# A graph network on one core: one-hots made once a group, a fused key compare, and another split of edge groups between two layers

## The chip, the core and the metric

One core of a Trainium2 chip runs the whole program as one launch. The metric is the device time of one execution in microseconds, the median over runs.

## The reference, cut to what matters

A graph of 6250 nodes with 206250 edges (sorted by `dst`; 128 features a node, 128 attributes an edge). Both layers gather node rows by edge and sum them by node:

```python
h = relu(layernorm(x))
deg = segment_sum(w, src) + 1                      # self loops added
msg = dinv[src] * w * dinv[dst] * (h @ kernel)[dst]
x = x + relu(segment_sum(msg, src) + bias)         # first layer
h = relu(layernorm(x))
m_fwd  = concat(h[src], edge_attr) @ W_fwd  + b_fwd    # summed by dst
m_back = concat(h[dst], edge_attr) @ W_back + b_back   # summed by src
agg = (segment_sum(m_fwd, dst) + segment_sum(m_back, src)) / count
x = x + layernorm(leaky(agg) + h) * gamma + beta   # second layer
```

So beside the sums over node rows there are two sums of edge attributes, by `src` and by `dst`, which both layers' passes collect.

## The kernel before

An edge group is 8 chunks of 128 edges (`J = 8`, `GE = 1024`); there are `NG = 202`. A supertile is 256 destination nodes; there are `SUPER = 25`. The stages, each a block of its own in which the five engines run their own instruction streams and meet at semaphores:

1. `setup_and_degrees` counts degrees, writes the edge records `d.rec` (source, destination, offset in the window, weight), the keys and the offsets.
2. `dst_lists` gathers, for each node, its edges' sources (50 columns) and, for the nodes from `S0` supertiles on, their weights (`near_w`, 2 x `DS` columns); POOL gathers them by indirect DMA, TensorE turns them.
3. `first_layer`, called the pass here. `G1 = GPI * (2 * DS + 1)` groups are walked in slots of `GPI` groups. For a chunk j of group g, VectorE makes three 128x128 matrices of ones and zeros: `spread_hot` (which window row an edge's destination is), `same` (which edges of the chunk have the same source) and `sum_hot` (like `spread_hot`, turned). TensorE spreads the window's rows over the edges (L838), adds the attributes by destination into the window bank (L852), and sums payload and attributes of edges with one source (L856, L857). ScalarE copies the sums (L929). POOL scatters the 128 rows of a chunk by an indirect DMA that adds in memory (L705). VectorE's `add_window` (L721) adds the window bank to `attr_sums`. The nodes of the last `DS` supertiles get their node sums in another way, by matrices: beside the groups of one slot, half a supertile is done: one-hots (`one_hots`, `weigh`; L776, L777, L782), batches of products that count edges for pairs (`pairs`, L888), turns (L866), a product with node rows (L878) and an addition to `gcn_t` (`add_up`, L791). These are dealt out over the slot's `C = GPI * J` chunk steps at a distance of `STRIDE = GPI // 2` steps. Weights of edges that go to those nodes are set to zero in the pass, so `G1` groups must cover all edges of the first `S0` supertiles.
4. `gcn_nodes` merges the four tables of sums and ends the first layer.
5. `dense_sums`, the second layer's node sums, by matrices for all 25 supertiles (called tiles here). The `NB = NG - G1` groups that are left run beside it: `PG` ahead of the first tile, then `GL = 4` beside each of `BT = (NB - PG) / GL` tiles; these lack payload and spread. Their tables are then loaded and merged (L1513, L1547) while the other tiles run.
6. `last_nodes` ends the second layer.

In each stream the order is fixed by the code. VectorE prepares group g + 1 (`prepare`) in the chunk steps of group g; step j waits until TensorE has summed chunk j of group g (`summed`, in the second layer `chunk_done`). SyncE loads a group's records (`rec`), offsets (`rel_b`), keys (`key_b`), window and attributes into two buffers each. ScalarE's `sums` hold two groups. A duplicate is told by an edge's earlier neighbours with its key (`before`): such an edge's row goes to a spare row.

## Time and profile before

| | |
|---|---|
| median of 3 runs | 4742.2 us (4732.38 to 4747.09) |
| the profiled execution: its time, its span | 4736.39 us, 4734.6 us |
| mean granted TensorE clock | 0.888 |
| busy: TensorE, VectorE, ScalarE, POOL | 73%, 79%, 39%, 60% |
| pass: first scatter to end of the last | 710.4 to 2702.0 us |
| second layer: first scatter, last tile's end | 2904.6, 4545 us |

Busy times count only work: semaphore, register and DMA-issuing instructions of an engine are left out, except POOL's indirect DMAs, whose span is the making of descriptors. "Idle before" a group is the time in which its engine did nothing ahead of its instructions, with what ended the idle. In a timeline the first number is the start in us, the second the duration; durations of VectorE overlap a little, so costs are read from start to start.

### The profile page before, as it was taken

The page shows a single profiled execution, that of the slowest core. Times are in us where ns is not written, and L with a number is a line of the kernel's source. Part 1 is how long each engine was busy: PE and PEld are TensorE (multiplying, and loading weights), DVE is VectorE, ACT ScalarE, POOL GpSimd, SP SyncE. Part 2 cuts the span into 40 slices and gives each one's busy share as a digit, 9 for nine tenths or more (in the row PEclk, how much of TensorE's full clock was granted, in tenths as well). Part 3 has the DMA queues.
Part 4 walks back from the last instruction along what each step waited for, and adds up shares of the span by engine and source line. Part 5 has one row for each costly group of instructions (what it writes and reads, how often), then busy time and mean ns, then how long its engine had stood idle before and what let it go on. Part 6 is the DMA issues. An engine that isn't in the chain of part 4 may idle for free. (4 is left out here: it accounts for less than half of the span.)

```text
span 4734.6 us, 104535 instructions
## 1 busy us (share of the span) xinstructions
PE 3462.1 (73%) x30910; PEld 2929.9 (62%) x31114; DVE 3722.4 (79%) x11962; ACT 1851.2 (39%) x4574; POOL 2819.5 (60%) x1705
## 2 busy tenths in 40 slices
PE   3555317888887888778888523798888888998955
PEld 3445217777776767677777422677777777776645
DVE  8999729998889888898899445887878777864527
ACT  1011004544444444444444313444444444455513
POOL 0000168888888888888888603787777777860000
PEclk8777659998989999999899766899999999999977
DMA  9990118888878777887788785455555555557031
GB/s 170 315 104 0 43 37 144 144 139 141 142 136 143 139 137 139 141 142 140 134 141 141 124 142 122 72 83 80 81 77 81 81 82 79 82 78 84 4 89 28
DMA packets 679953, 518.82 MB, mean 110 GB/s; under 512 B 305948, under 2 KB 592548, under 8 KB 677736
## 3 DMA queue, kind: packets, MB, share of 16 engines
q0 software_dynamic: 256640, 183.99, 34.6%
q1 hardware_dynamic: 422724, 327.85, 28.7%
q8 instruction: 263, 4.31, 0.4%
q14 instruction: 326, 2.67, 0.2%
HBM read 288.51 MB, written 249.53 MB: 114 GB/s over the span
## 5 line engine op out<-in xcount | busy, mean ns | idle before, releaser
L705 POOL DMA_INDIRECT gcn_sums<-fl_sums,fl_to_i x1008 | 1655.0, 1642 | 362.5 <-issue 160.2
L1531 POOL DMA_INDIRECT gcn_sums<-shared,ds_to_i x608 | 1038.0, 1707 | 486.6 <-ACT shared L1781 306.8
L929 ACT COPY fl_sums<-bank 128x256 f32<-128x256 f32 x1008 | 378.0, 376 | 662.2 <-PE bank L857 571.2
L1736 PE MATMUL bank<-ds_counts,ds_parts 128*128 128x256 bf16 x3675 | 595.5, 275 | 0.0
L852 PE MATMUL bank<-fl_sum_hot,fl_attrs 128*128 128x128 f32 x2016 | 404.9, 307 | 169.5 <-DVE attr_sums L721 169.4
L1805 ACT COPY ds_turned<-bank 128x1024 bf16<-128x1024 bf16 (+1 forms) x325 | 313.1, 963 | 537.7 <-PE bank L1721 534.7
L852 PEld LDWEIGHTS bank<-fl_sum_hot,fl_attrs 128*128 128x128 f32 x2016 | 328.3, 210 | 300.0 <-issue 259.9
L1769 ACT CAST ds_counts<-bank 128x392 bf16<-128x392 f32 x800 | 379.1, 491 | 234.9 <-PE bank L1679 222.0
L371 PE MATMUL bank<-places,row_hot 128*128 128x200 bf16 x1616 | 267.6, 292 | 255.4 <-DVE places L324 255.4
L856 PE MATMUL bank<-fl_pay,fl_same 128*128 128x128 f32 x2016 | 420.5, 292 | 30.2 <-DVE fl_same L741 23.1
L742 DVE SCALAR_TENSOR_TENSOR fl_earlier<-fl_key_b,fl_pat,before_me 128x128 bf16<-128x128 bf16 x1008 | 442.0, 439 | 0.0
L1756 PE MATMUL bank<-ds_turned,ds_now 128*128 128x512 bf16 (+1 forms) x1746 | 411.9, 365 | 10.9 <-issue 0.2
L838 PE MATMUL bank<-fl_window,fl_spread_hot 128*128 128x128 f32 x2016 | 294.9, 291 | 166.7 <-DVE fl_spread_hot L735 166.1
L922 ACT ACTIVATE fl_pay<-bank,fl_weight 128x128 f32<-128x128 f32 x1008 | 288.3, 369 | 326.6 <-PE bank L838 326.4
L857 PE MATMUL bank<-fl_attrs,fl_same 128*128 128x128 f32 x2016 | 410.8, 287 | 0.0
L1664 DVE TENSOR_TENSOR src_sums<-src_sums,bank 128x512 f32<-128x512 f32 (+1 forms) x325 | 212.1, 654 | 213.8 <-PE bank L1756 210.2
L838 PEld LDWEIGHTS bank<-fl_window,fl_spread_hot 128*128 128x128 f32 x2016 | 256.5, 199 | 196.2 <-DVE fl_spread_hot L735 164.1
L371 PEld LDWEIGHTS bank<-places,row_hot 128*128 128x128 bf16 x1616 | 194.0, 120 | 287.9 <-DVE places L324 276.3
L741 DVE TENSOR_SCALAR fl_same<-fl_key_b,fl_pat 128x128 f32<-128x128 bf16 x1008 | 351.8, 349 | 18.5 <-PE bank L857 16.0
L856 PEld LDWEIGHTS bank<-fl_pay,fl_same 128*128 128x128 f32 x2016 | 329.6, 204 | 54.1 <-issue 46.0
L735 DVE TENSOR_SCALAR fl_spread_hot<-fl_rel_b,part 128x128 f32<-128x128 bf16 x1008 | 359.1, 356 | 2.1 <-DMA fl_rel_b<-dst_offset 1.4
L1736 PEld LDWEIGHTS bank<-ds_counts,ds_parts 128*128 128x128 bf16 x3675 | 334.9, 99 | 29.7
(238 smaller groups left out, 8098.5 us busy)
## 6 DMA issues: line engine op xcount, KB each, us to landing
fl_attrs<-in_edge_attr SPq DMA_DIRECT2D x126, 512.0 KB, 4.6
shared<-in_edge_attr SPq DMA_DIRECT2D x150, 256.0 KB
fl_rel_b<-dst_offset SPq DMA_DIRECT2D x126, 256.0 KB
fl_key_b<-src_key SPq DMA_DIRECT2D x126, 256.0 KB
gcn_sums<-zeros SPq DMA_DIRECT2D x40, 640.0 KB
...
gcn_sums<-fl_sums,fl_to_i POOLq DMA_INDIRECT x1008
...
```

The source lines that it names most:

```text
L371: nc.tensor.matmul(hist[:, 0:4 * NT], row_hot[:, h, 0, j, :], col_w[:, h, j, :, :].rearrange("p s n -> p (s n)"), **ends)
L705: nc.gpsimd.indirect_dma_start(out=d.tab_gcn[j % K], out_offset=bass.IndirectOffsetOnAxis(ap=to_i[:, (GPI * kk + gi) % 4, j:j + 1], axis=0 ...
L742: counted = nc.vector.scalar_tensor_tensor(earlier[:, j, :], key_p[:, h, :, j], pat_f[:, j:j + 1], d.before_me[:], ALU.is_equal, ALU.mult, ...
L838: last = nc.tensor.matmul(row_bank[:, q * F:(q + 1) * F], spread_hot[:, half * U + q, :], window[:, h, :], start=True, stop=True)
L852: nc.tensor.matmul(win_bank[:, 0:P], attrs[:, h, jj, :], sum_hot[:, jj, :], start=(jj == 0), stop=(jj == J - 1))
L856: nc.tensor.matmul(sum_bank[j % 2][:, 0:F], same[:, j, :], pay[:, j // U, j % U, :], start=True, stop=True)
L857: nc.tensor.matmul(sum_bank[j % 2][:, F:2 * F], same[:, j, :], attrs[:, h, j, :], start=True, stop=True).then_inc(summed, 1)
L929: nc.scalar.copy(sums[:, h, j, :], sum_bank[j % 2][:, 0:2 * F]).then_inc(staged, 1)
L1531: nc.gpsimd.indirect_dma_start(out=d.tab_gcn[j % K].rearrange("n (two f) -> (n two) f", two=2), out_offset=bass.IndirectOffsetOnAxis(ap=to ...
L1736: ins = nc.tensor.matmul(row_bank[:, 0:2 * P], parts[:, tile, s, :], counts[:, h, tile, :, :].rearrange("p b q -> p (b q)"), start=(tile = ...
L1756: ins = nc.tensor.matmul(back_bank[v][:, 0:n], now[:, h, half, s, :], turned[:, v, half, 0:n], start=(half == 0 and s == 0), stop=(half == ...
L1769: nc.scalar.copy(to, pair_bank[batch % B][:, 0:PB * HH].rearrange("p (c k) -> p k c", c=PB)).then_inc(pair_copied, 1)
```

## The change

`S0` goes from 15 to 12 and `GPI` from 6 to 4, so `DS` is 13 instead of 10, the pass has 108 groups in 27 slots of 4 instead of 126 in 21 slots of 6, and 94 groups instead of 76 run in the second layer: `PG` = 6 ahead of it and 4 beside each of 22 tiles, not 18. `STRIDE` falls from 3 to 2.

On VectorE `same` is now made by the instruction that also counts: the compare is multiplied by `from_me` (key positions from the edge's own on) and summed, so `same` is triangular and the last edge of a key gets the whole sum; the separate `earlier` is gone. `spread_hot` is made by one instruction a group at step j = 2, `sum_hot` by one a group (`spot_sums`) at the group's first step, which waits until the group before is summed. The target indices need one instruction less in the pass.

```diff
@@ -62,14 +62,14 @@
 TILES = ROWS // P
 HI = -(-N // P)
 SUPER = TILES // 2
-S0 = 15
+S0 = 12
 DS = SUPER - S0
 DST0 = S0 * 2 * P
-GPI = 6
+GPI = 4
 G1 = GPI * (2 * DS + 1)
 NB = NG - G1
 GL = 4
-PG = 4
+PG = 6
 BT = (NB - PG) // GL
 PAIRS = P
 HH = 2 * HI
...
@@ -674,9 +674,11 @@
                     g, h = group(i, kk, gi), gi % 2
                     at_least(sp, to_ready, g - 1)
                     sp.sem_inc(load_turns, 1)
-                    sp.dma_start(flat(rec[:, h, :, :]), d.rec[bass.ds(g, 1), :, :].rearrange("o p r -> (o p) r")).then_inc(rec_in[h], 16)
                     sp.dma_start(flat(rel_b[:, h, :, :]), everywhere(d.dst_offset, g)).then_inc(rel_in[h], 16)
                     sp.dma_start(flat(key_b[:, h, :, :]), everywhere(d.src_key, g)).then_inc(key_in[h], 16)
+                    at_least(sp, sum_ready, g - 1)
+                    sp.sem_inc(load_turns, 1)
+                    sp.dma_start(flat(rec[:, h, :, :]), d.rec[bass.ds(g, 1), :, :].rearrange("o p r -> (o p) r")).then_inc(rec_in[h], 16)
                     at_least(sp, summed, J * (g - 1))
                     sp.sem_inc(load_turns, 1)
                     base = sp.value_load(d.base_i[0:1, bass.ds(g, 1)], min_val=0, max_val=N)
...
@@ -712,6 +714,12 @@
 
         @block.vector
         def _(dve):
+            def spot_sums(g, h):
+
+                at_least(dve, summed, J * g)
+                nc.vector.tensor_tensor(sum_hot[:], d.iota[:].unsqueeze(1).to_broadcast([P, J, P]), rec[:, h, 2, :].unsqueeze(2).to_broadcast([P, J, P]),
+                                        ALU.is_equal).then_inc(sum_ready, 1)
+
             def add_window(g):
 
                 at_least(dve, summed, J * (g + 1))
...
@@ -729,31 +737,24 @@
                     nc.vector.scalar_tensor_tensor(weight[:, h, :], rec[:, h, 1, :], DST0 - 0.5, rec[:, h, 3, :], ALU.is_lt, ALU.mult).then_inc(weight_ready, 1)
                     nc.vector.tensor_tensor(to_f[:], d.spare[:], rec[:, h, 0, :], ALU.subtract)
                     nc.vector.tensor_scalar(pat[:], rec[:, h, 0, :], PAT, 65536.0, ALU.add, ALU.mult).then_inc(step, 1)
-                    dve.wait_ge(rel_in[h], 16 * loads(i, kk, gi))
-                if ahead and j % U == 0:
-                    dve.wait_ge(row_ready, 2 * (g - 1) + j // U + 1)
-                nc.vector.tensor_scalar(spread_hot[:, j, :], rel_b[:, h, :, j], d.part[:, 0:1], None, ALU.is_equal).then_inc(spread_ready, 1)
-                if j == 0:
                     dve.wait_ge(key_in[h], 16 * loads(i, kk, gi))
-                    dve.wait_ge(step, 4 * g + 1)
+                    dve.wait_ge(step, 2 * g + 1)
                 if ahead:
                     dve.wait_ge(summed, J * (g - 1) + j + 1)
-                nc.vector.tensor_scalar(same[:, j, :], key_p[:, h, :, j], pat_f[:, j:j + 1], None, ALU.is_equal).then_inc(same_ready, 1)
-                counted = nc.vector.scalar_tensor_tensor(earlier[:, j, :], key_p[:, h, :, j], pat_f[:, j:j + 1], d.before_me[:],
-                                                         ALU.is_equal, ALU.mult, accum_out=before[:, j:j + 1])
+                nc.vector.scalar_tensor_tensor(same[:, j, :], key_p[:, h, :, j], pat_f[:, j:j + 1], d.from_me[:],
+                                               ALU.is_equal, ALU.mult, accum_out=later[:, j:j + 1]).then_inc(same_ready, 1)
+                if j == 2:
+                    dve.wait_ge(rel_in[h], 16 * loads(i, kk, gi))
+                    at_least(dve, row_ready, 2 * g)
+                    nc.vector.tensor_scalar(spread_hot[:], rel_b[:, h, :, :].rearrange("p q j -> p j q"), d.part[:, 0:1], None,
+                                            ALU.is_equal).then_inc(spread_ready, 1)
                 if j == J - 1:
-                    counted.then_inc(step, 1)
-                for jj in (range(4) if j == 3 else range(j, j + 1) if j > 3 else ()):
-                    nc.vector.tensor_scalar(sum_hot[:, jj, :], d.iota[:], rec[:, h, 2, jj:jj + 1], None, ALU.is_equal).then_inc(sum_ready, 1)
-                if j == J - 1:
-                    dve.wait_ge(step, 4 * g + 2)
-                    nc.vector.scalar_tensor_tensor(to_f[:], before[:], 0.0, to_f[:], ALU.is_gt, ALU.mult).then_inc(step, 1)
-                    dve.wait_ge(step, 4 * g + 3)
-                    nc.vector.tensor_tensor(to_f[:], to_f[:], rec[:, h, 0, :], ALU.add).then_inc(step, 1)
-                    dve.wait_ge(step, 4 * g + 4)
+                    dve.wait_ge(same_ready, J * (g + 1))
+                    nc.vector.scalar_tensor_tensor(to_f[:], later[:], 1.5, to_f[:], ALU.is_gt, ALU.mult).then_inc(step, 1)
+                    dve.wait_ge(step, 2 * g + 2)
                     for k in range(K):
                         at_least(dve, added[k], 16 * per_table * (g - 3))
-                    nc.vector.tensor_copy(to_i[:, (GPI * kk + gi) % 4, :], to_f[:]).then_inc(to_ready, 1)
+                    nc.vector.tensor_tensor(to_i[:, (GPI * kk + gi) % 4, :], to_f[:], rec[:, h, 0, :], ALU.add).then_inc(to_ready, 1)
                     dve.wait_ge(to_ready, g + 1)
 
             in_twos = lambda a: a.rearrange("p q (c two) -> p q c two", two=2)
...
@@ -804,6 +805,8 @@
                 more = not (isinstance(i, int) and i == DS)
                 for c in range(C):
                     gi, j = divmod(c, J)
+                    if j == 0:
+                        spot_sums(group(i, kk, gi), gi % 2)
                     if j == 0 and not (first and gi == 0):
                         add_window(group(i, kk, gi) - 1)
                     if not (last and gi == GPI - 1):
...
@@ -830,7 +833,7 @@
             def spread(i, kk, gi, half):
 
                 g, h = group(i, kk, gi), gi % 2
-                pe.wait_ge(spread_ready, J * g + U * (half + 1))
+                pe.wait_ge(spread_ready, g + 1)
                 if half == 0:
                     pe.wait_ge(window_in[h], 16 * loads(i, kk, gi))
                 at_least(pe, paid, J * g + U * half)
...
@@ -846,8 +849,7 @@
                     pe.wait_ge(attr_in[h], 16 * loads(i, kk, gi))
                 if j == 2:
                     at_least(pe, window_added, g)
-                if j >= 2:
-                    pe.wait_ge(sum_ready, ch + 1)
+                    pe.wait_ge(sum_ready, g + 1)
                 for jj in (range(3) if j == 2 else range(j, j + 1) if j > 2 else ()):
                     nc.tensor.matmul(win_bank[:, 0:P], attrs[:, h, jj, :], sum_hot[:, jj, :], start=(jj == 0), stop=(jj == J - 1))
                 pe.wait_ge(same_ready, ch + 1)
...
@@ -1449,9 +1450,10 @@
             pair_of_tiles(BT // 2 - 1, 1, True, False)
             if between:
                 between()
-            with eng.Fori(BT // 2, SUPER // 2 - 1) as i:
-                pair_of_tiles(i, 0, False, False)
-                pair_of_tiles(i, 1, False, False)
+            if BT < SUPER - 3:
+                with eng.Fori(BT // 2, SUPER // 2 - 1) as i:
+                    pair_of_tiles(i, 0, False, False)
+                    pair_of_tiles(i, 1, False, False)
             pair_of_tiles(SUPER // 2 - 1, 0, False, False)
             pair_of_tiles(SUPER // 2 - 1, 1, False, False)
             pair_of_tiles(SUPER // 2, 0, False, True)
...
@@ -1466,9 +1468,11 @@
                 g = G1 + q
                 at_least(sp, to_ready, q - 1)
                 sp.sem_inc(load_turns, 1)
-                sp.dma_start(rec[:, p, :, :].rearrange("p r j -> p (r j)"), d.rec[bass.ds(g, 1), :, :].rearrange("o p r -> (o p) r")).then_inc(rec_in[p], 16)
                 sp.dma_start(key_b[:, p, :, :].rearrange("p q j -> p (q j)"),
                              d.src_key[group_at(g)].rearrange("(o e) -> o e", o=1).to_broadcast([P, GE])).then_inc(key_in[p], 16)
+                at_least(sp, sum_ready, q - 1)
+                sp.sem_inc(load_turns, 1)
+                sp.dma_start(rec[:, p, :, :].rearrange("p r j -> p (r j)"), d.rec[bass.ds(g, 1), :, :].rearrange("o p r -> (o p) r")).then_inc(rec_in[p], 16)
                 for u in range(2):
                     at_least(sp, chunk_done, J * (q - 1) + U * (u + 1))
                     sp.sem_inc(load_turns, 1)
...
@@ -1585,22 +1595,17 @@
                     nc.vector.tensor_tensor(to_f[:], d.spare[:], rec[:, p, 0, :], ALU.subtract)
                     nc.vector.tensor_scalar(pat[:], rec[:, p, 0, :], PAT, 65536.0, ALU.add, ALU.mult).then_inc(step, 1)
                     dve.wait_ge(key_in[p], 16 * loads(i, h, gi))
-                    dve.wait_ge(step, 4 * q + 1)
+                    dve.wait_ge(step, 3 * q + 1)
                 if ahead:
                     dve.wait_ge(chunk_done, J * (q - 1) + j + 1)
-                nc.vector.tensor_scalar(same[:, j, :], key_p[:, p, :, j], pat_f[:, j:j + 1], None, ALU.is_equal).then_inc(same_ready, 1)
-                counted = nc.vector.scalar_tensor_tensor(earlier[:, j, :], key_p[:, p, :, j], pat_f[:, j:j + 1], d.before_me[:],
-                                                         ALU.is_equal, ALU.mult, accum_out=before[:, j:j + 1])
+                nc.vector.scalar_tensor_tensor(same[:, j, :], key_p[:, p, :, j], pat_f[:, j:j + 1], d.from_me[:],
+                                               ALU.is_equal, ALU.mult, accum_out=later[:, j:j + 1]).then_inc(same_ready, 1)
                 if j == J - 1:
-                    counted.then_inc(step, 1)
-                for jj in (range(4) if j == 3 else range(j, j + 1) if j > 3 else ()):
-                    nc.vector.tensor_scalar(sum_hot[:, jj, :], d.iota[:], rec[:, p, 2, jj:jj + 1], None, ALU.is_equal).then_inc(sum_ready, 1)
-                if j == J - 1:
-                    dve.wait_ge(step, 4 * q + 2)
-                    nc.vector.scalar_tensor_tensor(to_f[:], before[:], 0.0, to_f[:], ALU.is_gt, ALU.mult).then_inc(step, 1)
-                    dve.wait_ge(step, 4 * q + 3)
+                    dve.wait_ge(same_ready, J * (q + 1))
+                    nc.vector.scalar_tensor_tensor(to_f[:], later[:], 1.5, to_f[:], ALU.is_gt, ALU.mult).then_inc(step, 1)
+                    dve.wait_ge(step, 3 * q + 2)
                     nc.vector.tensor_tensor(to_f[:], to_f[:], rec[:, p, 0, :], ALU.add).then_inc(step, 1)
-                    dve.wait_ge(step, 4 * q + 4)
+                    dve.wait_ge(step, 3 * q + 3)
                     for k in range(K):
                         at_least(dve, added[k], 16 * (J // K) * (q - 3))
                     nc.vector.tensor_scalar(to_i[:, (PG + gi) % 4, :], to_f[:], 2.0, 1.0, ALU.mult, ALU.add).then_inc(to_ready, 1)
...
@@ -1609,6 +1614,8 @@
             def beside_step(i, h, c):
 
                 gi, j = divmod(c, J)
+                if j == 0:
+                    spot_sums(behind(i, h, gi), gi % 2)
                 if j == 0 and gi > -PG:
                     add_window(behind(i, h, gi) - 1)
                 if not (isinstance(i, int) and 2 * i + h == BT - 1 and gi == GL - 1):
```

VectorE in the pass, where one group ends and the next begins, before (names: `fl_` tiles of `first_layer`; L782 are the weighted one-hots, L721 is the window addition):

```order
L756 CAST fl_to_i<-fl_to_f 128x8
L791 TENSOR_TENSOR gcn_t<-gcn_t,bank 128x512
L782 TENSOR_TENSOR fl_hi_w<-fl_hi_hot,fl_twos 128x784 x3
L718 TENSOR_LOAD base_i
L718 ISA x2
L721 ISA
L721 TENSOR_TENSOR attr_sums<-attr_sums,bank 128x128
L729 SCALAR_TENSOR_TENSOR fl_weight<-fl_rec 128x8
L730 TENSOR_TENSOR fl_to_f<-spare,fl_rec 128x8
```

and after:

```order
L757 TENSOR_TENSOR fl_to_i<-fl_to_f,fl_rec 128x8
L783 TENSOR_TENSOR fl_hi_w<-fl_hi_hot,fl_twos 128x784 x3
L720 TENSOR_TENSOR fl_sum_hot<-iota,fl_rec 128x1024
L726 TENSOR_LOAD base_i
L726 ISA x2
L729 ISA
L729 TENSOR_TENSOR attr_sums<-attr_sums,bank 128x128
L737 SCALAR_TENSOR_TENSOR fl_weight<-fl_rec 128x8
```

The one-hot of 1024 elements stands between the weighted one-hots and the window addition, and the addition of a product (L791) has moved away.

VectorE in the second layer, the same place of a group beside a tile, before (`shared` holds keys, `same` and `sum_hot`; L1578 is the window addition):

```order
L1606 TENSOR_SCALAR ds_to_i<-ds_to_f 128x8
...
L1575 ISA
L1575 TENSOR_LOAD base_i
L1575 ISA x2
L1578 ISA
L1578 TENSOR_TENSOR attr_sums<-attr_sums,bank 128x128
L1585 TENSOR_TENSOR ds_to_f<-spare,ds_rec 128x8
L1586 TENSOR_SCALAR ds_pat<-ds_rec 128x8
L1588 ISA
...
L1591 TENSOR_SCALAR shared<-shared,ds_pat 128x128
L1592 SCALAR_TENSOR_TENSOR ds_earlier,ds_before<-shared,ds_pat,before_me 128x128
```

and after:

```order
L1611 TENSOR_SCALAR ds_to_i<-ds_to_f 128x8
L1579 TENSOR_TENSOR shared<-iota,ds_rec 128x1024
L1585 ISA
L1585 TENSOR_LOAD base_i
L1585 ISA x2
L1588 ISA
L1588 TENSOR_TENSOR attr_sums<-attr_sums,bank 128x128
L1595 TENSOR_TENSOR ds_to_f<-spare,ds_rec 128x8
L1596 TENSOR_SCALAR ds_pat<-ds_rec 128x8
L1598 ISA
...
L1601 SCALAR_TENSOR_TENSOR shared,ds_later<-shared,ds_pat,from_me 128x128
```

The spot one-hot of the whole group (L1579) now stands ahead of the window addition, and one fused compare follows where two instructions stood.

SyncE in the pass, the loads of one group, before:

```order
L677 DMA fl_rec<-edge_records 128x32
L678 DMA fl_rel_b<-dst_offset 128x1024
L679 DMA fl_key_b<-src_key 128x1024
L682 TENSOR_LOAD base_i
L682 ISA x2
L683 ISA
L683 DMA fl_window<-g 128x128
L684 DMA fl_attrs<-in_edge_attr 128x1024
```

and after:

```order
L677 DMA fl_rel_b<-dst_offset 128x1024
L678 DMA fl_key_b<-src_key 128x1024
L681 DMA fl_rec<-edge_records 128x32
L684 TENSOR_LOAD base_i
L684 ISA x2
L685 ISA
L685 DMA fl_window<-g 128x128
L686 DMA fl_attrs<-in_edge_attr 128x1024
```

The load of `rec` has moved behind offsets and keys, and behind a wait for the spot one-hot.

## Rows read from the trace of the kernel before

**Rows 1.** Stretches: busy us of PE, PEld, DVE, ACT, POOL; clock, DMA share, GB/s.

```profile
1000.00:2500.00 1500.00, 1218.95 (x10149) 1067.35 (x10145) 1332.04 (x5242) 698.41 (x1953) 1244.29 (x760) 0.93 0.80 140
3100.00:4000.00 900.00, 797.80 (x7448) 646.59 (x7564) 719.62 (x2390) 413.35 (x718) 699.83 (x419) 0.98 0.52 80
```

**Rows 2.** Groups of the page: POOL's scatters, pass and second layer.

```profile
L705 POOL DMA_INDIRECT gcn_sums<-fl_sums,fl_to_i x1008 | 1655.0, 1642 | 362.5 <-issue 160.2
L1531 POOL DMA_INDIRECT gcn_sums<-shared,ds_to_i x608 | 1038.0, 1707 | 486.6 <-ACT shared L1781 306.8
```

**Rows 3.** Timeline of POOL: first and last scatter of the pass.

```profile
710.36 2.03 POOL L705 DMA_INDIRECT gcn_sums<-fl_sums,fl_to_i  x1 [25.78 <-DVE fl_to_i L756]
...
2700.46 1.56 POOL L705 DMA_INDIRECT gcn_sums<-fl_sums,fl_to_i  x1 [0.30 <-issue]
```

**Rows 4.** Timeline: gathers of the node lists, and VectorE beside them.

```profile
586.10 0.94 POOL L446 DMA_INDIRECT li_near<-near,li_near_row_i  x1 [0.30 <-issue]
587.34 3.19 POOL L446 DMA_INDIRECT li_near<-near,li_near_row_i  x1 [0.30 <-issue]
...
586.23 3.49 DVE L501 TENSOR_TENSOR li_outside<-iota,li_first_at 128x3200 f32<-128x3200 f32 x1
```

**Rows 5.** Timeline of VectorE in the pass, parts of one group.

```profile
1510.28 0.57 DVE L776 TENSOR_TENSOR fl_hi_hot<-fl_numbers,fl_twos 128x784 bf16<-128x784 bf16 x1
...
1511.37 0.34 DVE L735 TENSOR_SCALAR fl_spread_hot<-fl_rel_b,part 128x128 f32<-128x128 bf16 x1
1511.61 0.33 DVE L741 TENSOR_SCALAR fl_same<-fl_key_b,fl_pat 128x128 f32<-128x128 bf16 x1
1511.86 0.44 DVE L742 SCALAR_TENSOR_TENSOR fl_earlier<-fl_key_b,fl_pat,before_me 128x128 bf16<-128x128 bf16 x1
...
1512.22 0.94 DVE L747 TENSOR_SCALAR fl_sum_hot<-iota,fl_rec 128x128 f32<-128x128 f32 x4
1513.06 0.67 DVE L791 TENSOR_TENSOR gcn_t<-gcn_t,bank 128x512 f32<-128x512 f32 x1
1513.65 1.51 DVE L782 TENSOR_TENSOR fl_hi_w<-fl_hi_hot,fl_twos 128x784 bf16<-128x784 bf16 x3
1515.09 0.32 DVE L735 TENSOR_SCALAR fl_spread_hot<-fl_rel_b,part 128x128 f32<-128x128 bf16 x1
```

**Rows 6.** Timeline of TensorE in the pass, parts of one group.

```profile
1508.73 0.39 PE L857 MATMUL bank<-fl_attrs,fl_same 128*128 128x128 f32 x2
1508.95 0.60 PE L866 MATMUL bank<-ident,fl_mat 128*128 128x128 f32 x4
1509.39 1.02 PE L878 MATMUL bank<-fl_turned,fl_g_tile 128*128 128x512 f32 x2
1510.25 0.39 PE L852 MATMUL bank<-fl_sum_hot,fl_attrs 128*128 128x128 f32 x2
...
1510.92 0.68 PE L888 MATMUL bank<-fl_hi_w,fl_lo_hot 128*128 128x98 bf16 x12
1511.44 0.45 PE L852 MATMUL bank<-fl_sum_hot,fl_attrs 128*128 128x128 f32 x2
```

**Rows 7.** Timeline of ScalarE: row copies ending tiles 0, 17, 21, 24.

```profile
3053.23 0.38 ACT L1826 COPY ds_row_stage<-bank 128x256 f32<-128x256 f32 x1
...
4212.95 0.38 ACT L1826 COPY ds_row_stage<-bank 128x256 f32<-128x256 f32 x1
...
4410.90 0.37 ACT L1826 COPY ds_row_stage<-bank 128x256 f32<-128x256 f32 x1 [2.56 <-PE bank L1736]
...
4545.22 0.37 ACT L1826 COPY ds_row_stage<-bank 128x256 f32<-128x256 f32 x1 [2.56 <-PE bank L1736]
```

**Rows 8.** Waits from 3000 to 4200 us: total us, times, longest.

```profile
PE bank L1698 <- DVE attr_sums L1578: 48.8, 35, 1.9
```

**Rows 9.** Timeline of POOL, last two merges; the merges' landing.

```profile
4322.15 5.54 POOL L1547 DMA_DIRECT2D shared<-gcn_sums  x2 [27.30 <-DMA shared<-gcn_sums]
...
DMA to landing us min/median/max: 29.0/29.7/32.2
```

15 lines of the change are left out of this document (9 added, 6 removed).

## Prediction

> **What bounds the kernel now.** I read the busy times by stage first [rows 1]. In the pass over the edges (first layer) VectorE is busy 89%, TensorE 81% and POOL 83%: by these shares VectorE looks like the bound. The groups of POOL [rows 2] and its rows in order of time [rows 3] say otherwise. A scatter keeps POOL 1.56 us, and 0.30 us of idle stand before it even where it waits for nothing but its issue, as before the last one. So the 1008 scatters of the pass need 1008 x 0.30 = 302 us of the 362.5 us of idle; 25.8 us stand before the first one, and only 34 us are left as true waits. From the first scatter at 710.4 to the end of the last at 2702.0 are 1991.7 us, made of 1008 x 1.56 = 1572.5, 302.4 of gaps, 82.5 by which scatters last longer than 1.56 (mean 1.642), and 34 of waits. The pass is bound by the issue of scatters, 15.8 us for a group of 8, with VectorE close behind.
>
> Why scatters are stretched: the gathers of the node lists last 0.94 us, but 3.19 us beside VectorE's two-input instruction of 3.49 us [rows 4]. POOL waits for such an instruction to end.
>
> Beside the second layer TensorE is busy 89% [rows 1] and POOL 0.78 + 419 x 0.30 / 900 = 92%; both are close. A tile with four groups takes (4212.95 - 3053.23) / 17 = 68.2 us, the four tiles after them 49.5 us each, the last three 134.3 us together [rows 7]. So a group costs 15.8 us in the pass and (68.2 - 49.5) / 4 = 4.7 us beside the second layer. This difference is what moving groups is worth.
>
> **The change, part by part.** Scatters in all stay 1616. The pass has 864 instead of 1008, the second layer 752 instead of 608.
>
> *Node lists.* POOL gathers six more columns of weights at the pitch from 586.10 to 587.34, 1.24 us [rows 4]: 7.5 us, and TensorE and VectorE see the last one later. A fourth batch of four tiles adds about 1.5. Together +9 (7 to 12). The added compare in the setup is under 1 us.
>
> *The pass, POOL.* 864 x 1.86 = 1607 us at least. Stretch: unchanged per scatter it would be 71; if it belongs to the one-hots of the matrices (now 26 half supertiles, not 20) it is 82.5 x 1.3 = 107. The new one-hot of 1024 elements with two inputs is priced by the row of 3200 elements, 3.49 x 1024 / 3200 = 1.12, with its start 1.2 us [rows 4]; once a group it costs POOL between 0 and 108 x 1.2 = 130. VectorE's other two-input work in the pass, mostly short, cost 82.5 us; I take 110 in all, nearer the low end, because one such instruction in 16 us meets at most one scatter. Waits were 34; I take 60, for the reason below. Sum 1607 + 110 + 60 = 1777, against 1991.7: **-215**. Bounds: 1607 + 71 + 30 = 1708 (-284), and 1607 + 237 + 100 = 1944 (-48).
>
> In the Trainium skill, SBUF — State Buffer, section "Who interferes with whom", two-input instructions contend with GpSimd instructions that read SBUF, yet its probe of tensor_tensor did not stall the making of descriptors. By that last remark the new one-hot would cost POOL nothing and my 110 would be about 84. Row 3.19 against 0.94 in this trace says that indirect DMAs are held, so the measurement decides.
>
> *The pass, VectorE.* From start to start a chunk's spread one-hot takes 0.24 us, its key compare 0.25, the masked count 0.36 and a spot one-hot 0.84 / 4 = 0.21 [rows 5]. The fused compare replaces two by one of 0.36. Spread and spot one-hots become one instruction a group each, about 1.2 us; the spread one might run at double rate and take 0.7. With about 1 us of small ones a group goes from 8 x 1.06 + 1 = 9.5 us to 8 x 0.36 + 2.4 + 1 = 6.3. The matrix work of a half supertile stays: 8 x (1.09 + 1.44) and 13 x 0.59, 29 us with its copies [rows 5]. A slot (half supertile) was 6 x 9.5 + 29 = 86 of 95.6 us and becomes 4 x 6.3 + 29 = 54.
>
> *The pass, TensorE.* A chunk is four fp32 products of 0.22 us; a turn 0.44, a product 0.86, a batch of pairs 0.52 [rows 6]. A slot becomes 32 x 0.89 + 13 x 1.30 + 16 x 0.52 = 54 us, before 68.
>
> *Against each other.* POOL needs (1607 + 110) / 27 = 63.6 us a slot, so it stays the bound. But the cover is thinner. Batches of pairs now come every second chunk, and VectorE must have the next one-hots within three chunks, not five. The spot one-hot is made only when the last chunk of the group before is summed, so at a group's turn VectorE runs compare, two small ones, three weighted one-hots and then the spot one-hot: 0.36 + 0.7 + 1.44 + 1.2 + 0.3 = 4.0 us, while TensorE reaches the third chunk after 0.45 + 1.30 + 0.45 + 0.89 + 0.52 = 3.6. The register load of the window's base, which waited about 0.9 us alone, now lies under the one-hot. A full group then takes 14.4 + about 1 on TensorE, a slot 58 to 62: under 63.6, but near enough that I double the waits. Behind such a wait of TensorE stand the sums that ScalarE copies and POOL scatters; two groups of buffers cover it. SyncE's loads of rec now wait for the spot one-hot of two groups ago; they are needed a group, 16 us, later: nothing. The first scatter comes about 4 us earlier, since the first group's preparation falls from about 11 us: -4.
>
> *Second layer.* Four tiles turn from plain to accompanied: 4 x 68.2 - (4410.90 - 4212.95) = 273 - 198 = **+75** [rows 7]. I leave an accompanied tile at 68.2: VectorE loses 4 x 2.5 us of work, but at a group's turn its chain is as long as before (1.3 saved on compare and base, 1.2 added), and TensorE's wait there is 48.8 us in 1200 [rows 8]. Two more groups go ahead of the first tile: 16 scatters are 32 us of POOL (2.0 each); the sums' buffers let TensorE run about a group and a half ahead, so +14 (5 to 32).
>
> *Behind the groups.* The merges of the tables end at 4322.15 + 5.54 + 29.7 = 4357.4, 144 us after the last accompanied tile [rows 7, 9]. Seven plain tiles covered them; three take 134 and about 3 of storing. **+7**.
>
> **Sum.** 9 - 215 - 4 + 75 + 14 + 7 = -114, from the profiled execution's 4736.4 to 4622. The median of the runs shown is 5.8 above that execution, so I predict **4628**.
>
> **Rivals.**
> 1. *The stretch and the waits do not grow* (18%). Then a scatter keeps its 1991.7 / 1008 = 1.976 us and the pass is 1707, -285; the total 4558. For it: VectorE has less to do in a slot (54 of 64 us, before 86 of 96). Against: 30% more matrix one-hots and a long new one.
> 2. *The spot one-hot lands on the path beside the second layer* (17%). TensorE waits there already for the window [rows 8]; 1.2 us more at every one of 94 turns would be 113 and eat the gain (4741), half of it gives 4685. For it: the one-hot was ready a group ahead before. Against: the lighter compare and the hidden register load.
> 3. *The slot of the pass becomes bound by VectorE and TensorE in turn* (8%), at the third chunk of each group and at the pairs. It decides from a slot of 65.8 + 114 / 27 = 70 us on. At 73 us the pass is 1971, -21, and the total 4822: slower. For it: both engines hold 54 us of work and wait for each other in order. Against: each would have to idle a quarter of the time, where VectorE now idles 11%.
> 4. *It does nothing* (5%): less stretch relief and longer tiles balance, 4742.
>
> My forecast, 4570 to 4690, holds 52%. With parts of the rivals the range for 8 in 10 is 4560 to 4705. A difference under 0.3%, 14 us, can't be told from none: faster 0.87, same 0.05, slower 0.08.
>
> **What the profile after would show.** POOL's scatters of the pass 864, mean 1.66 to 1.72 us, first to last about 1777 us, with idle near 0.30 each; below 1.65 rival 1 is right. VectorE's share in the pass falls little or not at all, though a group costs it a third less, since matrices come more often. TensorE's waits for the window or the spot one-hot: about 1 us a group; above 2 us, with POOL idle far over 0.30, rival 3. Rows of the row copy by ScalarE: 68 us apart; 70 or more is rival 2. The merges' last landing behind the last tile shows the 7. Wrong would make me above all a scatter that costs another time than 1.99 to 2.06 us with its gap and waits.

## The result, and the profile after

The changed kernel takes 4618.77 us (median of 4 runs, 4610.76 to 4623.39); the kernel before took 4742.52 in the same session. The ratio is 0.974, 95% interval 0.9719 to 0.9761. The forecast was 4628, the range 4560 to 4705. Between the two profiled executions, 4736.39 and 4623.39 us, lie 113.0 us; the sum of the prediction had 114.

The stretches that answer to [rows 1], in the same columns:

```profile
1000.00:2500.00 1500.00, 1263.22 (x11417) 1095.04 (x11415) 1172.37 (x3295) 757.40 (x2047) 1232.10 (x726) 0.95 0.78 135
3100.00:4000.00 900.00, 809.73 (x7454) 646.07 (x7453) 601.75 (x1582) 407.98 (x707) 710.94 (x413) 0.96 0.51 79
```

In the second layer VectorE has become idler (720 us busy before, 602 now) and TensorE and POOL a little busier. This stretch gains nothing by it, as the tiles below show. In the pass VectorE is busy 78% instead of 89%: part of the room was filled again by matrix work, which comes in 27 slots instead of 21.

POOL's scatters, groups of the page (busy, mean ns, idle before), to be held against [rows 2]:

```profile
L707 POOL DMA_INDIRECT gcn_sums<-fl_sums,fl_to_i x864 | 1470.1, 1702 | 307.4 <-DMA gcn_sums<-fl_sums,fl_to_i 151.7
L1535 POOL DMA_INDIRECT gcn_sums<-shared,ds_to_i x752 | 1303.3, 1733 | 533.4 <-ACT shared L1787 319.9
```

And in POOL's timeline the first and last scatter of the pass, and the first of the second layer:

```profile
716.56 2.04 POOL L707 DMA_INDIRECT gcn_sums<-fl_sums,fl_to_i  x1 [25.26 <-ACT fl_sums L931]
...
2467.27 1.58 POOL L707 DMA_INDIRECT gcn_sums<-fl_sums,fl_to_i  x1 [0.30 <-issue]
...
2674.05 1.57 POOL L1535 DMA_INDIRECT gcn_sums<-shared,ds_to_i  x1 [205.21 <-ACT shared L1787]
```

The pass is 2468.85 - 716.56 = 1752.3 us long. It is read as in the prediction: 864 x 1.56 = 1348 of plain issue, 864 x 0.30 = 259 of gaps, 1470.1 - 1348 = 122 by which scatters last longer than 1.56, and the rest, 307.4 - 25.3 - 259 = 23, waits. I call the 122 the **stretch** below (before 82).

ScalarE's row copies, which end tiles 0, 21 and 24 (answering to [rows 7]):

```profile
2835.09 0.38 ACT L1832 COPY ds_row_stage<-bank 128x256 f32<-128x256 f32 x1
...
4293.69 0.38 ACT L1832 COPY ds_row_stage<-bank 128x256 f32<-128x256 f32 x1
...
4427.52 0.37 ACT L1832 COPY ds_row_stage<-bank 128x256 f32<-128x256 f32 x1 [2.56 <-PE bank L1742]
```

An accompanied tile takes (4293.69 - 2835.09) / 21 = 69.5 us, not 68.2. These are the two stretches of accompanied tiles, before and after (columns of [rows 1]):

```profile
3053.23:4212.95 1159.72, 1034.65 (x9694) 839.06 (x9845) 931.39 (x3086) 537.83 (x937) 918.09 (x544) 0.99 0.53 81
2835.09:4293.69 1458.60, 1315.86 (x12163) 1051.12 (x12161) 979.84 (x2566) 666.03 (x1157) 1162.83 (x675) 0.97 0.51 80
```

A tile has 60.9 us of busy TensorE before and 62.7 after, 7.4 and 6.8 us of idle. (Before, 1.6% of the records are missing; e1 below, which lacks as many, has 62.3 and 7.1.) So the 1.3 us are not more waiting: TensorE is slower at its work. Its granted clock stands at the lower of its two levels, 1.2 GHz and not 2.4, for 27 of 1160 us before and for 96 of 1459 us after.

Then the last merges of the tables, and SyncE's first load of the stage behind them (timelines of POOL and SyncE):

```profile
4400.34 5.55 POOL L1551 DMA_DIRECT2D shared<-gcn_sums  x2 [26.76 <-DMA shared<-gcn_sums]
...
4438.72 0.83 SPq L1988 DMA_DIRECT2D n_w<-in_L_gnn_W_back  x2
```

Counted to that load, the stage begins 4438.7 - 4427.5 = 11.2 us behind the last tile, 7.6 before.

Where the 113 us came from, with the steps of the prediction:

| step | forecast | measured |
|---|---|---|
| node lists, up to the first scatter | +5 | +6.2 |
| pass, first scatter to last | -215 | -239.4 |
| first layer's end | 0 | +2.6 |
| two more groups ahead of tile 0 | +14 | +12.4 |
| tiles 0 to 24, by the row copies | +75 | +100.4 |
| merges behind the tiles | +7 | +3.6 |
| last stage | 0 | +1.1 |
| sum | -114 | -113.1 |

The total is right partly because two errors of 25 us stand against each other.

### The profile page after: what moved, and what is told of

It reads as the page before. It is cut to its first block and busy times, and to the rows that moved or that the text cites. A ratio compares the mean times of both kernels' runs of the same rounds, so it can differ in the third digit from the quotient of the medians.

```text
span 4621.6 us, 103887 instructions
## 1 busy us (share of the span) xinstructions
PE 3497.9 (76%) x32143; PEld 2940.4 (64%) x32143; DVE 3319.0 (72%) x8239; ACT 1864.9 (40%) x4498; POOL 2905.8 (63%) x1711
## 3 DMA queue, kind: packets, MB, share of 16 engines
q0 software_dynamic: 256832, 174.75, 34.5%
## 5 line engine op out<-in xcount | busy, mean ns | idle before, releaser
L707 POOL DMA_INDIRECT gcn_sums<-fl_sums,fl_to_i x864 | 1470.1, 1702 | 307.4 <-DMA gcn_sums<-fl_sums,fl_to_i 151.7
L1535 POOL DMA_INDIRECT gcn_sums<-shared,ds_to_i x752 | 1303.3, 1733 | 533.4 <-ACT shared L1787 319.9
L744 DVE SCALAR_TENSOR_TENSOR fl_same<-fl_key_b,fl_pat,from_me 128x128 f32<-128x128 bf16 x864 | 374.1, 445 | 132.0 <-PE bank L859 110.2
L1704 PE MATMUL bank<-shared 128*128 128x128 f32 x1504 | 307.7, 309 | 116.7 <-DVE attr_sums L1588 88.1
L858 PE MATMUL bank<-fl_pay,fl_same 128*128 128x128 f32 x1728 | 351.3, 286 | 44.0 <-issue 28.2
L1601 DVE SCALAR_TENSOR_TENSOR shared<-shared,ds_pat,from_me 128x128 f32<-128x128 bf16 x752 | 312.2, 443 | 92.3 <-PE bank L1706 74.5
L1706 PE MATMUL bank<-shared 128*128 128x128 f32 x1504 | 320.7, 297 | 72.1 <-DVE shared L1601 49.2
L890 PE MATMUL bank<-fl_hi_w,fl_lo_hot 128*128 128x98 bf16 x4992 | 293.5, 209 | 105.0 <-DVE fl_hi_w L783 87.8
L854 PE MATMUL bank<-fl_sum_hot,fl_attrs 128*128 128x128 f32 x1728 | 327.4, 292 | 46.1 <-DVE attr_sums L729 45.8
L890 PEld LDWEIGHTS bank<-fl_hi_w,fl_lo_hot 128*128 128x128 bf16 x4992 | 260.0, 99 | 129.8 <-issue 111.4
L880 PE MATMUL bank<-fl_turned,fl_g_tile 128*128 128x512 f32 (+1 forms) x676 | 334.3, 576 | 3.6 <-DVE gcn_t L792 1.3
```

What stands on the lines that cost most here:

```text
L707: nc.gpsimd.indirect_dma_start(out=d.tab_gcn[j % K], out_offset=bass.IndirectOffsetOnAxis(ap=to_i[:, (GPI * kk + gi) % 4, j:j + 1], axis=0 ...
L744: nc.vector.scalar_tensor_tensor(same[:, j, :], key_p[:, h, :, j], pat_f[:, j:j + 1], d.from_me[:], ALU.is_equal, ALU.mult, accum_out=late ...
L854: nc.tensor.matmul(win_bank[:, 0:P], attrs[:, h, jj, :], sum_hot[:, jj, :], start=(jj == 0), stop=(jj == J - 1))
L858: nc.tensor.matmul(sum_bank[j % 2][:, 0:F], same[:, j, :], pay[:, j // U, j % U, :], start=True, stop=True)
L880: nc.tensor.matmul(prod_bank[:, 0:n], g_tile[:, old, :], turned[:, (old + b) % 2, 0:n], start=True, stop=True).then_inc(prod_ready, 1)
L890: last = nc.tensor.matmul(pair_bank[at][:, c * HH:(c + 1) * HH], lo_hot[:, go % 2, q, :], hi_w[:, go % 2, m, q, :], start=(m == 0), stop=( ...
```

## The experiments

The change has two parts that can be told apart: VectorE's new code (the fused compare; one instruction a group for `spread_hot` and for `sum_hot`), and the new split of groups. Twelve kernels took them apart. "Pass" is first scatter to end of the last, "second" the same in the second layer; the stretch is the scatters' busy time over 1.56 us each. Both are read from one profiled execution, which lay up to 13 us from the median of its kernel (e10 13 below, e14 13 above), so stage times that differ by less say little.

| kernel | total, median | ratio to before, 95% | pass | stretch | waits | second |
|---|---|---|---|---|---|---|
| before | 4742 | | 1991.7 | 82 | 34 | 1322.0 |
| changed | 4618.8 | 0.9719-0.9761 | 1752.3 | 122 | 23 | 1631.5 |
| e1 new code, old split | 4788.9 | 1.0084-1.0118 | 2027.7 | 130 | 23 | 1335.3 |
| e2 old code, new split | 4774.2 | 1.0060-1.0094 | 1915.1 | 124 | 184 | 1615.4 |
| e3 `sum_hot` in 8, same place | 4691.4 | 0.9867-0.9921 | 1776.0 | 101 | 68 | 1674.2 |
| e4 `sum_hot` twice (pass) | 4727.9 | 0.9961-0.9984 | 1851.8 | 155 | 90 | 1630.5 |
| e5 `sum_hot` early (pass) | 4660.5 | 0.9817-0.9849 | 1786.8 | 156 | 23 | 1627.9 |
| e8 half of the pass's scatters | 4551.0 | one run | 1682.8 | 76 of 432 | - | 1630.7 |
| e9 `spread_hot` in 8, same place | 4663.3 | 0.9813-0.9871 | 1797.5 | 132 | 59 | 1625.2 |
| e10 fused compare and split alone | 4562.2 | 0.9608-0.9663 | 1729.0 | 85 | 37 | 1583.8 |
| e11 e10 and `spread_hot` per group | 4609.5 | 0.9715-0.9787 | 1777.6 | 150 | 21 | 1598.3 |
| e12 fused compare alone, old split | 4720.6 | 0.9944-0.9981 | 1985.1 | 58 | 52 | 1313.3 |
| e13 one unread long one-hot more | 4634.5 | 0.9762-0.9804 | 1768.2 | 148 | 13 | 1628.6 |
| e14 five unread short ones more | 4635.6 | 0.9763-0.9805 | 1778.7 | 155 | 17 | 1628.8 |

Waits are the pass less issue, gaps of 0.30 and stretch. Differences of totals in the text below are differences of the ratios times 4740 us, since the kernel before had a median of 4738 to 4743 us from session to session.

**e1, the code without the split.**

```diff
-S0 = 12          -GPI = 4          -PG = 6
+S0 = 15          +GPI = 6          +PG = 4
```

> The changed kernel with its new VectorE code, but with the old split: S0 = 15, GPI = 6, PG = 4, so 1008 scatters in the pass and 76 groups beside the second layer. Theory A (the pass is bound by POOL's issue of scatters, and what the change brings is 18 groups moved from 15.8 us to 4.7 us each): the code alone brings little; at 1.98 to 2.03 us a scatter the pass takes 1995 to 2045 us and the total lies between 4725 and 4790, likeliest 4745, with VectorE's share in the pass down from 89% to about 73%. Theory B (VectorE bound the pass and the lighter code is the gain): the pass falls from 1992 us by 80 us or more and the total to 4620 to 4670.

It is 1.0% slower than before. VectorE got room (69% busy from 1000 to 2300 us, before 89%) and nobody used it. The group of the page, and TensorE's waits from 1000 to 2300 us (total, times, longest):

```profile
L707 POOL DMA_INDIRECT gcn_sums<-fl_sums,fl_to_i x1008 | 1702.0, 1689 | 349.3 <-DMA gcn_sums<-fl_sums,fl_to_i 182.9
```

```profile
PE bank L858 <- ACT fl_sums L931: 185.2, 132, 4.8
```

TensorE, which hardly ever waited for ScalarE's copies, now waits 185 us in 1300 for them (0.7 before): the copies need a buffer that POOL has scattered. This is how a bound on POOL looks from TensorE. The pass is even 36 us longer, since the mean scatter rose from 1642 to 1689 ns. Theory A holds, theory B (VectorE bound the pass) falls. e1 alone mixes the room with what the one-hots per group cost; e12 below, without them, says the same.

**e2, the split without the code.** The same three numbers in the kernel before.

> The kernel before with its old VectorE code, but with the new split: S0 = 12, GPI = 4, PG = 6, 108 groups in the pass and 94 beside the second layer. VectorE's work in a slot is then 4 x 9.5 + 29 = 67 us against POOL's 32 x 1.976 = 63.2 us. Theory A says that the two parts of the change need each other: VectorE becomes the bound of the pass at 68 to 73 us a slot, the pass takes 1840 to 1970 us, the total is 4700 to 4800, likeliest 4750. If the split alone is the gain (VectorE's code has nothing to do with it), the pass is 1710 to 1760 and the total 4600 to 4640.

```profile
L705 POOL DMA_INDIRECT gcn_sums<-fl_sums,fl_to_i x864 | 1471.5, 1703 | 470.6 <-issue 198.1
```

```profile
PE bank L888 <- DVE fl_hi_w L782: 157.2, 125, 2.2
```

Slower too, by 0.8%. POOL now idles 471 us, of which 184 are true waits, and TensorE waits 157 us in 1300 for the one-hots of the matrices. A slot takes 1915 / 27 = 70.9 us: VectorE bounds it, as its 67 us of work say. So each part alone loses and both together win.

**e8, the floor.** What VectorE and TensorE need when POOL is not the bound. Half of the pass's scatters are left out, so its sums are incomplete (the indices of rows and buffers, not shown, follow):

```diff
-                    for j in range(J):
+                    for j in range(K):
...
-                        pool.wait_ge(staged, J * g + j + 1)
+                        pool.wait_ge(staged, J * g + 2 * j + 2)
```

> The changed kernel, in which the pass scatters the sums of every second chunk only: 432 of 864 scatters are left out, so the first layer's source sums and half of the attributes' source sums are incomplete. POOL then needs about 33 us a slot and can't be the bound. Theory A (POOL's issue bounds the pass, VectorE and TensorE in turn need 58 to 62 us a slot): the pass, first scatter to end of the last, falls from 1752 us to 1570 to 1680, likeliest 1610. Rival (VectorE and TensorE bound it at 64.9 us a slot): the pass stays within 20 us of 1752.

The pass is 1682.8 us, 62.3 a slot, 3 us over the bounds that were expected: POOL was the bound of the changed kernel's 64.9, but by 4% only. The forecast had 58 to 62 for this floor. It is a single run, and half of the scatters' memory traffic is gone with them.

**e5, the spot one-hot a group ahead.**

```diff
+                if j == 4:
+                    spot_sums(g, h)
...
-                    if j == 0:
-                        spot_sums(group(i, kk, gi), gi % 2)
```

> The changed kernel, but in the pass sum_hot has two buffers and is made by the same one instruction at step j = 4 of the group before instead of at the group's own first step. At a group's turn VectorE then has 1.2 us less ahead of the one-hots of the matrices. Theory A (POOL's issue bounds the pass; its true waits there are only about 22 us): TensorE's waits for the matrices' one-hots (87.8 us) fall by half, POOL's waits by 0 to 15 us, the total is 4600 to 4620, likeliest 4613. Rival (the place of the one-hot is on the path of the pass): the pass falls by 40 us or more, the total is under 4580.

Both missed: 44 us slower, not a few faster. The waits stayed at 23 and the stretch rose by 34 us, which is the whole 34.5 that the pass lost. So moving one instruction of 1.2 us to another step changed what scatters cost. This made theory C, that a long VectorE instruction holds the scatter being issued, tested by the next four.

**e3, sum_hot in eight instructions** at the same place:

```diff
-                nc.vector.tensor_tensor(sum_hot[:], d.iota[:].unsqueeze(1)..., rec[:, h, 2, :]..., ALU.is_equal).then_inc(sum_ready, 1)
+                for jj in range(J):
+                    spot = nc.vector.tensor_scalar(sum_hot[:, jj, :], d.iota[:], rec[:, h, 2, jj:jj + 1], None, ALU.is_equal)
+                spot.then_inc(sum_ready, 1)
```

> The changed kernel, but sum_hot is written at the same place by eight instructions of one chunk each instead of one of 1024 elements, in the pass and beside the second layer. New theory C, from the traces so far (a long VectorE instruction holds POOL's scatter that is being issued: between 1000 and 2300 us of the changed kernel 60 of 642 scatters that overlap the new sum_hot most are 0.52 us longer each, 31 us, while 7 beside the old short ones lost 0.9 us in all): what the scatters of the pass last over 1.56 us falls from 122 us by 25 to 42, the total is 4575 to 4600. Rival D (any VectorE work of the same place and amount holds POOL alike): that sum stays at 110 to 135 us, the total is 4610 to 4630, since VectorE now works about 0.5 us longer a group.

Missed by both theories. The stretch fell by 22 us, a little less than theory C's 25 to 42, but the total rose by 73 us. What VectorE does at a group's turn grew by 0.5 us, and both stages pay for it: waits in the pass +45, the second layer +43, 0.45 us for each of 94 turns. TensorE's waits from 3100 to 4000 us say where; first this kernel, then e10, in which `sum_hot` is made ahead of the turn (the changed kernel has 30.5):

```profile
PE bank L1706 <- DVE attr_sums L1590: 41.6, 17, 3.3
```

```profile
PE bank L1690 <- DVE attr_sums L1573: 20.2, 13, 1.7
```

**e9, spread_hot in eight instructions** at its place, step j = 2:

```diff
-                    nc.vector.tensor_scalar(spread_hot[:], rel_b[:, h, :, :].rearrange("p q j -> p j q"), d.part[:, 0:1], None,
-                                            ALU.is_equal).then_inc(spread_ready, 1)
+                    for jj in range(J):
+                        spread = nc.vector.tensor_scalar(spread_hot[:, jj, :], rel_b[:, h, :, jj], d.part[:, 0:1], None, ALU.is_equal)
+                    spread.then_inc(spread_ready, 1)
```

> The changed kernel, but spread_hot is written at the same place (step j = 2) by eight instructions of one chunk each instead of one of 1024 elements with one tensor input. Theory C: the excess of the pass's scatters falls from 122 us by 20 to 36 us (54 scatters of 642 are 0.49 us longer each beside it), the total is 4580 to 4605. Rival (only an instruction with two tensor inputs holds POOL, and this one has one): excess and total stay, 4610 to 4630.

Missed by both theories: 48 us slower, the stretch not smaller (132) and the waits up by 36. To the start of the next instruction, eight short ones in a row take 2.07 us and the long one 1.08 (medians), and they hold POOL no less.

**e4, sum_hot twice** in the pass:

```diff
+                nc.vector.tensor_tensor(unread[:], d.iota[:].unsqueeze(1)..., rec[:, h, 2, :]..., ALU.is_equal)
                 nc.vector.tensor_tensor(sum_hot[:], d.iota[:].unsqueeze(1)..., rec[:, h, 2, :]..., ALU.is_equal).then_inc(sum_ready, 1)
```

> The changed kernel, but in the pass the instruction that makes sum_hot is run twice, the first time into a buffer that nobody reads. Theory C: the excess of the pass's scatters over 1.56 us grows by as much again as the first costs, 30 to 60 us from 122, and the total to 4650 to 4690. If the long instruction cost POOL nothing, the excess stays at 115 to 130 us; since VectorE has room in a slot the total then stays at 4615 to 4640.

110 us slower, well over what theory C said. The stretch grew by 32, inside its bounds, but the waits grew by 67: 1.2 us more at each of 108 turns is nearly all on the path, as the floor of 62.3 a slot makes one expect.

**e10, the fused compare and the split alone.** Both one-hots go back to one instruction a chunk at their old steps. SyncE's load of `rec` loses the wait for the spot one-hot; but its order, behind offsets and keys, stays that of the changed kernel here and in e11 and e12, unlike what the expectations say. The fused compare also brings its shorter making of the target indices:

```diff
+                if ahead and j % U == 0:
+                    dve.wait_ge(row_ready, 2 * (g - 1) + j // U + 1)
+                nc.vector.tensor_scalar(spread_hot[:, j, :], rel_b[:, h, :, j], d.part[:, 0:1], None, ALU.is_equal).then_inc(spread_ready, 1)
...
+                for jj in (range(4) if j == 3 else range(j, j + 1) if j > 3 else ()):
+                    nc.vector.tensor_scalar(sum_hot[:, jj, :], d.iota[:], rec[:, h, 2, jj:jj + 1], None, ALU.is_equal).then_inc(sum_ready, 1)
```

> The kernel before with the new split and the fused compare alone: spread_hot and sum_hot by chunk at their old steps, SyncE's loads in their old order. VectorE then needs 4 x (8 x 0.81 + 1) + 29 = 59 us a slot. Theory C: the excess of the pass's scatters is 40 to 80 us instead of 122, the slot comes near to 62 us, the least that VectorE and TensorE need by the run with half of the scatters; the pass takes 1680 to 1725 us, the total is 4545 to 4590, faster than the changed kernel. Rival (room on VectorE is what the per-group one-hots bring, and without it the waits come back): the pass takes 1750 us or more, the total 4615 to 4700.

4562.2 us: the fastest complete kernel of this study, about 50 us under the changed one; the two intervals lie clear of each other. The total is as expected; the pass (1729) and the stretch (85) each lie 4 us over their bounds. Its group, and the row copies of tiles 0 and 21:

```profile
L705 POOL DMA_INDIRECT gcn_sums<-fl_sums,fl_to_i x864 | 1432.4, 1658 | 321.8 <-issue 133.4
```

```profile
2815.05 0.38 ACT L1818 COPY ds_row_stage<-bank 128x256 f32<-128x256 f32 x1
...
4224.19 0.38 ACT L1818 COPY ds_row_stage<-bank 128x256 f32<-128x256 f32 x1
```

A tile takes 67.1 us here, 69.5 in the changed kernel, 68.3 in e2. So beside the second layer the fused compare gains 1.2 us a tile and `sum_hot` at the turn gives back 2.4. Of the 2.4, 0.9 are more idle of TensorE and 1.5 more busy time for the same products. The changed kernel has the longer waits for the window addition: 21 of them, as many as tiles, are over 1.5 us, up to 2.64, where e10 has at most 1.68 and the kernel before 1.91. Within 2.5 us behind 12 of these 21 waits the clock falls to 1.2 GHz. Behind this one it stays there from 2958.28 to 2961.69 us (TensorE, changed kernel):

```profile
2957.55 1.01 PE L1704 MATMUL bank<-shared 128*128 128x128 f32 x6 [2.38 <-DVE attr_sums L1588]
```

At the lower level stand 96 us of the 21 tiles in the changed kernel, 24 in e10. If work takes twice the time there, this is (96 - 24) / 2 = 36 of the 50 us between them, an estimate. In the nine kernels with `sum_hot` at the turn of the second layer, 6 to 18 falls stand so behind a wait over 1.5 us, in the five others at most one. No run held the clock still, so what the waits alone cost is not shown.

**e12, the fused compare alone**: e10 at the old split. The edit is shown against e10.

```diff
-S0 = 12          -GPI = 4          -PG = 6
+S0 = 15          +GPI = 6          +PG = 4
```

> The kernel before with the fused compare alone: old split (1008 scatters in the pass), one-hots by chunk at their old steps. Theory A (POOL's issue bounds the pass at the old split): the pass is 1960 to 1990 us (before: 1992), the second layer gains some 25 us in its 76 groups as it gained 32 in 94 by the same edit at the new split; the total is 4690 to 4730, likeliest 4705. Rival (the fused compare would have brought most of the gain without the split): the total is under 4650.

In the total as expected, 0.4% faster; the second layer gained 9 us, not 25. VectorE is busy 78% from 1000 to 2300 us, before 89%, and the pass is 7 us shorter: POOL bounds it. With e2 and e10 this is a table of two by two: the split alone +36 us, the fused compare alone -18, both -173. Then the one-hots per group add about 50 (e10 to the changed kernel), and at the old split 66 (e12 to e1).

**e11, spread_hot per group** added to e10:

```diff
-                nc.vector.tensor_scalar(spread_hot[:, j, :], rel_b[:, h, :, j], d.part[:, 0:1], None, ALU.is_equal).then_inc(spread_ready, 1)
+                if j == 2:
+                    nc.vector.tensor_scalar(spread_hot[:], rel_b[:, h, :, :].rearrange("p q j -> p j q"), d.part[:, 0:1], None,
+                                            ALU.is_equal).then_inc(spread_ready, 1)
```

> The changed kernel with sum_hot by chunk at its old steps in both layers, and SyncE's loads in their old order; of the new one-hots only the one spread_hot instruction a group is left. The run with both by chunk took 4562 us, the changed kernel 4619, and with sum_hot off the group's turn the second layer was 48 us shorter (first scatter to end of the last). Theory E (what costs is sum_hot at the group's turn, where TensorE waits for it in the second layer): the second layer's stretch is 1584 us within 10, the total 4560 to 4585. Rival (the long spread_hot, which holds POOL's scatters, is the larger part): the pass stays at 1750 us or more and the total at 4585 to 4610.

The rival is right: `spread_hot` per group alone lengthens the pass by 48.6 us and the stretch by 65. `sum_hot` per group, added to this, shortens the pass by 25 and lengthens the second layer by 33. Theory E missed: e11 has e10's code beside the second layer, yet is 14.5 us longer there. The clock is at its lower level for 58 us of e11's 21 tiles and 24 of e10's; why is open.

**e13 and e14, the twins.** A one-hot into an unread buffer, off the turn, once as one instruction, once as five. The twins differ in more than length: the long one reads two tensors, the short ones one tensor and a scalar for each partition:

```diff
+                if j == 5:
+                    nc.vector.tensor_tensor(unread[:], d.iota[:].unsqueeze(1)..., rec[:, h, 2, :]..., ALU.is_equal)
```

```diff
+                if j >= 3:
+                    nc.vector.tensor_scalar(unread[:, j, :], d.iota[:], rec[:, h, 2, j:j + 1], None, ALU.is_equal)
```

> The changed kernel, and in the pass one more instruction a group at step j = 5: a one-hot of 1024 elements into a buffer that nobody reads, 1.2 us, away from the group's turn. Its twin does the same amount of VectorE time in five short ones. Theory C (one long VectorE instruction holds the scatter that is being issued): the excess of the pass's scatters over 1.56 us grows by 30 to 60 us from 122 and the total is 4650 to 4690, and both are at least 20 us above the twin's. Rival F (what counts is VectorE's time in the slot, which runs near its floor of 62.3 us, however it is cut): both twins lose the same, within 15 us.

> The twin: the changed kernel, and in the pass five more instructions a group, one at each of the steps j = 3 to 7: a one-hot of one chunk each (128 elements) into a buffer that nobody reads, 5 x 0.21 = 1.05 us of VectorE. Theory C: the excess of the pass's scatters stays at 115 to 140 us and the total is 4620 to 4650. Rival F: the same loss as its twin with one long instruction, within 15 us.

Both lose about 20 us, and their medians are 1.1 us apart. That is what rival F expected; theory C wanted 20 us or more between them. Rival F's reason is only half of it: the loss stands in the stretch (+26, +33) and not in waits, which went down.

What a scatter waits for can be read in the changed kernel's timelines, POOL first in each pair:

```profile
1103.60 2.61 POOL L707 DMA_INDIRECT gcn_sums<-fl_sums,fl_to_i  x1 [0.30 <-issue]
```

```profile
1103.55 1.22 DVE L720 TENSOR_TENSOR fl_sum_hot<-iota,fl_rec 128x1024 f32<-128x1024 f32 x1
1104.69 0.28 DVE L729 TENSOR_TENSOR attr_sums<-attr_sums,bank 128x128 f32 x1
```

```profile
1500.18 2.02 POOL L707 DMA_INDIRECT gcn_sums<-fl_sums,fl_to_i  x1 [0.30 <-issue]
```

```profile
1500.72 1.39 DVE L749 TENSOR_SCALAR fl_spread_hot<-fl_rel_b,part 128x1024 f32<-128x1024 bf16 x1
1502.04 0.67 DVE L792 TENSOR_TENSOR gcn_t<-gcn_t,bank 128x512 f32<-128x512 f32 x1
```

The first scatter starts 0.05 us into `sum_hot`, and ends at 1106.21, 1.5 us after VectorE has gone on to the next instruction (1104.69): it stood still until then and then took its usual time. The second meets `spread_hot` halfway, and ends 0.16 us after VectorE goes on (1502.20, 1502.04). So a scatter has a point at its start and one later where it waits for the VectorE instruction in progress. I put the first point alone as a rule: the duration is 1.56 us, or 1.51 plus the time until VectorE's next instruction starts, whichever is longer. It gives 223 of the 297 scatters between 1000 and 1600 us to 0.06 us, where 1.56 for all would give 171, and 99 of the 126 that last over 1.62.

Not every VectorE instruction holds a scatter. The stretch of the pass, by the instruction in progress when a scatter starts, in rounded us (the fourth row: `spread_hot` follows, and the scatter starts in the addition before it, L792 in the changed kernel):

| | changed | e5 | e10 | e11 | e13 | e14 |
|---|---|---|---|---|---|---|
| matrices' one-hots | 47 | 52 | 65 | 78 | 42 | 57 |
| fused compare | 21 | 13 | 9 | 26 | 28 | 32 |
| `spread_hot` at the start | 18 | 10 | 2 | 14 | 13 | 22 |
| `spread_hot` at the later point | 0 | 42 | 0 | 21 | 0 | 0 |
| `sum_hot` | 31 | 32 | 3 | 3 | 36 | 40 |
| the unread one-hot | | | | | 27 | 1 |
| others, none | 6 | 7 | 5 | 8 | 2 | 4 |

This answers most of what the totals left open. e5 lost its 34 us because 50 scatters that start beside L792 now meet `spread_hot` at the later point; in the changed kernel none of 120 does. In e10 the two one-hots by chunk cost scatters 5 us, in the changed kernel by group 48. In e13 the long unread instruction lengthens 49 of the 54 scatters that start in it; in e14 the short ones lengthen none of 53, and there the loss stands beside the other instructions. So theory C holds for what such an instruction does itself, and fails for the total, since each edit also shifts where the other instructions meet the scatters. These are readings of the traces: no run fixed the phase.

## Why the prediction was right, and where it was not

- **The bound.** "The pass is bound by the issue of scatters, 15.8 us for a group of 8, with VectorE close behind": shown by e1 and e12 (room on VectorE gains nothing or 7 us), e8 (half of the scatters out: -70 us), and e2 (with the old code VectorE takes over at 70.9 us a slot).
- **The price of a group.** 15.8 us in the pass against 4.7 beside the second layer carried the forecast. In the changed kernel they are 1752.3 / 108 = 16.2 and, with the old plain tile, (69.5 - 49.5) / 4 = 5.0. Of plain tiles it has only the last three, 133.8 us together, before 134.3.
- **The pass, POOL: the waits.** "I take 60" is the term that was mis-sized: they were 23. The stall forecast for TensorE is there, 68.6 us in 73 waits for the matrices' one-hots between 1000 and 2300 us, but the two groups of sums ahead of POOL took it up. Doubling the waits for a thin cover was wrong; e4 shows that with 1.2 us more a turn they do grow, by 67.
- **The pass, POOL: the stretch.** "110 in all", measured 122, on the wrong ground. I priced `sum_hot` alone, as the two-input instruction, near nothing, and `spread_hot` at nothing. In the trace scatters lose 31 us beside the one and 18 beside the other; beside the matrices' one-hots, which most of the 110 was meant for, they lose 47, less than the 55 before. With the old code at the new split (e2) that last part is 101 of 124. The sum was right by luck.
- **The pass, VectorE.** 6.3 us a group and 54 a slot hold: VectorE is 82% busy from 1000 to 2300 us, 53 of 64.9 us. But only the fused compare was needed for that room. With the one-hots by chunk VectorE is 89% busy in e10, which is faster. (A slot before was 1991.7 / 21 = 94.8 us, not 95.6.)
- **Second layer, tiles.** Leaving an accompanied tile at 68.2, since 1.3 us are saved at a turn and 1.2 added, failed by 1.3 us a tile, 26 in all. The two do cancel in kind, as e2, e10 and the changed kernel show (68.3, 67.1, 69.5), but the one-hot at the turn costs twice what the compare saves. What the sum had no term for is the clock: TensorE's idle did not grow against the kernel before (7.4 and 6.8 us a tile), its time at 1.2 GHz did, from 1.6 to 4.6 us a tile.
- **Rival 2** is thus real as a mechanism: about 33 to 48 us of the second layer (e11, e10), more than half of it by the clock, if the estimate under e10 holds. It stayed small in the total since the fused compare paid for a part.
- **Rival 1** (no growth of stretch and waits): half true. The waits did not grow, the mean scatter did, 1.642 to 1.702. **Rival 3** (a slot of 70 us or more) is what e2 is; with the new code it did not come about.
- Node lists, the two groups ahead and the merges were right within 4 us each.
